# Attention in a fused four-layer kernel: the softmax maxima as contraction rows brought by DMA, and parts stored pair by pair

## The reference

```python
x = x + tanh(g_xattn[0]) * delay_attention(layernorm(x), ctx)
x = x + tanh(g_ffn[0]) * top1_experts(layernorm(x))      # 8 experts
def attention(query, kv):                                # the third layer
    q = (query @ w_q.T).reshape(B, T_q, 16, 8)
    k = (kv @ w_k.T).reshape(B, T_kv, 16, 8)
    v = (kv @ w_v.T).reshape(B, T_kv, 16, 8)
    attn = softmax(einsum('bqhd,bkhd->bhqk', q, k) * 8 ** -0.5, axis=-1)
    return einsum('bhqk,bkhd->bqhd', attn, v).reshape(B, T_q, 128) @ w_o.T
x = x + tanh(g_xattn[1]) * attention(layernorm(x), ctx)
x = x + tanh(g_ffn[1]) * top2_experts(layernorm(x))      # 8 experts
```

## Time and profile before

| | |
|---|---|
| median of 3 runs | 371.15 us (360.84, 371.15, 374.12) |
| profiled execution | 360.57 us |
| its span, first to last instruction | 358.8 us |
| PE busy / DVE / ACT / POOL | 299.6 / 199.5 / 119.0 / 155.1 us |
| mean granted clock of TensorE | 0.92 of full speed |
| experts of the second layer end | 134 us into the span |
| first scores of the attention loop | 157.1 us |
| last addition to x of the attention | 253.2 us |

### The profile page before, as it was taken

One profiled execution on the slowest core, in us unless ns is written; L12 is line 12 of the kernel. 1 busy time (PEld: TensorE's weight loads), 2 busy tenths in 40 slices (PEclk: granted clock), 3 DMA queues, 4 the chain that ended last, 5 costly groups with the idle time before them and its releaser, 6 DMA issues.

```text
span 358.8 us, 8553 instructions
## 1 busy us (share of the span) xinstructions
PE 299.6 (83%) x3060; PEld 253.8 (71%) x3060; DVE 199.5 (56%) x602; ACT 119.0 (33%) x268; POOL 155.1 (43%) x330
## 2 busy tenths in 40 slices
PE   6799978799999983646899899998138999999990
PEld 2556668599999981234688788885125999989980
DVE  4826859344444443723586566663793566656650
ACT  1234144111221110226556455555320333323320
POOL 8550000777776431164364344341017417775521
PEclk9699997999999996969999999999655999999996
DMA  7907995269999964061396959911147999999900
GB/s 204 354 2 207 405 303 172 60 234 266 389 400 310 223 132 132 26 133 18 92 161 132 139 125 142 213 47 32 29 119 256 316 339 399 357 322 300 333 24 7
DMA packets 55023, 70.47 MB, mean 196 GB/s; under 512 B 4555, under 2 KB 44918, under 8 KB 54982
## 3 DMA queue, kind: packets, MB, share of 16 engines
q1 hardware_dynamic: 48006, 59.63, 55.2%
q0 software_dynamic: 3664, 8.73, 9.6%
q10 hardware_dynamic: 3312, 1.58, 1.7%
HBM read 58.95 MB, written 10.96 MB: 195 GB/s over the span
## 4 chain that ended last, share of the span: by engine, by line
PE 55%; DVE 14%; DMA 14%; issue 5%; SPq 4%; ACT 3%; POOL 3%; POOLq 0%; DVEq 0%; ACTq 0%
PE bank L1147 7%; PE bank L974 6%; PE pairA L964 5%; PE pairB L964 5%; PE pairB L1137 4%; DMA qs<-rows_d_d,inv_i 4%; PE pairA L1137 4%; DMA qs<-qparts_d 3%; PE pairB L1490 3%; PE pairA L1481 3%; PE pairB L1491 3%; PE bank L1506 3%; DMA qparts_d<-parts 3%; SPq L1441 2%; SPq L1262 2%
## 5 line engine op out<-in xcount | busy, mean ns | idle before, releaser
L1563 DVE TENSOR_REDUCE maxi<-pairA 128x8 f32<-128x1024 f32 x32 | 39.0, 1220 | 27.5 <-PE pairA L1481 27.3
L1543 ACT ACTIVATE prob<-pairB 128x1024 f32<-128x1024 f32 x32 | 32.8, 1024 | 33.9 <-PE pairB L1491 33.9
L1043 POOL DMA_INDIRECT qs<-rows_b_d,inv_i x23 | 22.4, 973 | 44.0 <-DVE inv_i L723 37.4
L1147 PE MATMUL bank<-wring,prob 128*128 128x128 f32 x312 | 41.3, 276 | 0.0
L1147 PEld LDWEIGHTS bank<-wring,prob 128*128 128x128 f32 x312 | 37.9, 192 | 0.0
L1491 PE MATMUL pairB<-mrow,pick 72*128 72x128 bf16 x256 | 32.0, 219 | 0.0
L1048 POOL DMA_INDIRECT back_d<-ysb,inv_i x23 | 22.6, 984 | 16.8 <-DVE ysb L1009 15.0
L1232 POOL DMA_INDIRECT out_x<-qs,inv_i x16 | 15.8, 987 | 27.1 <-DVE qs L1196 24.9
L1222 POOL DMA_INDIRECT qs<-rows_d_d,inv_i x16 | 15.5, 968 | 27.8 <-DVE inv_i L787 23.2
L1598 POOL TENSOR_TENSOR mparts<-zeros,maxi 128x8 bf16<-128x8 f32 x32 | 7.6, 237 | 41.9 <-DVE maxi L1563 41.9
L1490 PE MATMUL pairB<-qs,ks 72*128 72x128 bf16 x192 | 24.1, 219 | 1.2 <-ACT mrow L1548 1.2
(11 more groups left out here) (306 smaller groups left out, 667.1 us busy)
## 6 DMA issues: line engine op xcount, KB each, us to landing
wring<-in_wts SPq DMA_DIRECT2D x39, 514.0 KB, 7.0
wring<-in_wts SPq DMA_DIRECT2D x23, 768.0 KB, 7.4
ks<-kparts_d SPq DMA_DIRECT2D x18, 192.0 KB
qs<-qparts_d SPq DMA_DIRECT2D x18, 192.0 KB
kparts_d<-parts SPq DMA_DIRECT2D x4, 384.0 KB, 4.0
ctx_s<-kparts_d SPq DMA_DIRECT2D x6, 192.0 KB
qparts_d<-parts SPq DMA_DIRECT2D x3, 384.0 KB, 7.0
ctxT<-qparts_d SPq DMA_DIRECT2D x6, 192.0 KB
```

The costliest lines, as they stand in the source:

```text
L1043: eng.indirect_dma_start(out=xt[:, t.x, :], out_offset=None, in_=rows_d["b"], in_offset=bass.IndirectOffsetOnAxis(ap=inv_i[:, 0, t.k:t.k + ...
L1147: j = eng.matmul(bank[1 + i % 2][:, 0:D], act[:, i % 2, c_, :], wring[:, i % RW, o:o + D], start=(c_ == 0), stop=(c_ == C1 - 1))
L1543: eng.activation(prob[:, at.half(2), :, :].rearrange("p h t -> p (h t)"), pairB[:, :, :].rearrange("p a t -> p (a t)"), ACT.Exp)\
L1563: eng.reduce_max(maxi[:, at.half(0), :], pairA[:, :, :].rearrange("p a (h t) -> p (a h) t", t=T), AX).then_inc(s("mx"), 1)
```

## The change

- `pick` and its 8 matmuls per unit go. The three parts of the negated maxima become contraction rows 72 to 74 (`SM` = 75) of the query side: for each unit SP sends `mrow` (now 24 x 128) by a DMA into rows 72 to 74 of the slot (`rows_of`). The key side has ones there (`ONES` read as two bf16), set by a memset for slots 0 and 1 and copied by DMA to the others (`load_ones`).
- Transposed scores move from two to four steps behind the scores, and what follows them moves by two steps (`LAG` 9 to 11). `mparts` and `mrow` have four buffers.
- Five slots for pairs. Slots 3 and 4 lie in `wring`, the ring of expert weights, and their keys are loaded after the experts of the second layer.
- `kparts_d` and `qparts_d` have one block for each pair, so that a load is 24 rows of 4096 contiguous bf16; writes are one DMA for each pair and go in runs of 256 bf16. SP's list weaves writes, loads and `rows_of` by unit.
- Ahead of the loop: 17 DVE instructions for the inverse deviation become 7 (`spread`) plus a power and a product on POOL (`root`); statistics are taken in another order; a first exponential of one column goes ahead of the norms on ACT; the warm matmuls are 44 and 20 (10 and 14 before), and the 44 no longer wait for x. The norms of chunks 2 to 4 are given to other engines and steps, and the work of these chunks to other steps.

```diff
+    SM = SK + PARTS
+    ROWS = 4
...
-    WARM = (20, 22, 30, 10, 10, 14, 2, 3, 2, 4)
+    WARM = (20, 22, 30, 10, 44, 20, 2, 3, 2, 4)
...
-        kparts_d = scratch("kparts_d", (2 * PARTS - 1, HD * H, NTOK), bf16)
-        qparts_d = scratch("qparts_d", (PARTS, HD * H, NTOK), bf16)
+        kparts_d = scratch("kparts_d", (NB // 2, 2 * PARTS - 1, HD * H, 2 * T), bf16)
+        qparts_d = scratch("qparts_d", (NB // 2, PARTS, HD * H, 2 * T), bf16)
...
-        pick = sb("pick", [SK, HU, T], bf16)
...
-        mparts = sb("mparts", [128, 2, SK], bf16)
-        mrow = sb("mrow", [SK, 2, T], bf16)
+        mparts = sb("mparts", [128, ROWS, PARTS * HU], bf16)
+        mrow = sb("mrow", [PARTS * HU, ROWS, T], bf16)
...
+        def spread(eng, c, lo, hi):
+
+            me, mo, ve, vo = (st[:, lo:hi, k] for k in (1, 4, 2, 5))
+            less, diff, total, var, u, mean = (lnv[:, k, lo:hi] for k in (0, 1, 2, 4, 5, 6))
+            eng.tensor_tensor(diff, me, mo, ALU.subtract)
+            eng.tensor_tensor(total, me, mo, ALU.add)
+            c.link(eng.scalar_tensor_tensor(var, ve, D * EPS, vo, ALU.add, ALU.add))
+            eng.tensor_scalar(mean, total, 0.5, None, ALU.mult)
+            eng.tensor_scalar(less, total, -0.5, None, ALU.mult)
+            c.link(eng.scalar_tensor_tensor(u, diff, 0.25, diff, ALU.mult, ALU.mult))
+            eng.scalar_tensor_tensor(var, var, 1.0 / D, u, ALU.mult, ALU.add).then_inc(s("spread"), 1)
+
+        def root(eng, nth, lo, hi):
+
+            eng.wait_ge(s("spread"), nth)
+            eng.tensor_tensor(lnv[:, 3, lo:hi], lnv[:, 4, lo:hi], neg_half[:, lo:hi], ALU.pow).then_inc(s("root"), 1)
+            eng.wait_ge(s("root"), nth)
+            eng.tensor_tensor(lnv[:, 7, lo:hi], lnv[:, 0, lo:hi], lnv[:, 3, lo:hi], ALU.mult).then_inc(s("rstd"), 1)
...
-        SLOTS = 3
+        SLOTS = 5
...
+        spare_ring = wring[:, 2:RW, :].rearrange("p r w -> p (r w)")
+        spare_slot = [wide(spare_ring[:, n * H * T:(n + 1) * H * T]) for n in range(4)]
+
+        qslot = [qs[0:SM, 0, :, :], qs[0:SM, 1, :, :], wide(ctxT[:, :]), spare_slot[0], spare_slot[1]]
+        kslot = [ks[0:SM, 0, :, :], ks[0:SM, 1, :, :], wide(ctx_s[:, :, :].rearrange("p b d -> p (b d)")), spare_slot[2], spare_slot[3]]
+
+        def load_ones(eng, slot):
+            eng.dma_start(kslot[slot][SK:SM, :, :], kslot[0][SK:SM, :, :]).then_inc(s("ones"), 16)
...
+        def load_rows(eng, slot, parts_d, pair, step):
+
+            for j in range(PARTS):
+                v = parts_d[pair, j * step:j * step + PARTS].rearrange("i (d h) t -> (i d) (h t)", h=H)
+                rows = slot[pair % SLOTS][j * PARTS * HD:(j + 1) * PARTS * HD, :, :]
+                eng.dma_start(rows.rearrange("p h t -> p (h t)"), v).then_inc(s(f"qk{pair % SLOTS}"), 16)
...
-            for j in range(PARTS):
-                v = kparts_d[j:j + PARTS].rearrange("i (d h) t -> (i d) h t", h=H)[:, :, pair * 2 * T:(pair + 1) * 2 * T]
-                eng.dma_start(kslot[pair % SLOTS][j * PARTS * HD:(j + 1) * PARTS * HD, :, :], v).then_inc(s(f"qk{pair % SLOTS}"), 16)
...
+            eng.activation(gt[:, 0, 0:1], zeros[:, 0:1], ACT.Exp)
...
             c.link(take(0))
-            rstd(eng, c, RSTD_C0, 0, GB)
+            spread(eng, c, 0, GB)
+            take(1)
+            eng.wait_ge(s("root"), 1)
             norm_dve(eng, 0).then_inc(s("xnD"), 1)
             norm_dve(eng, 2).then_inc(s("xnD"), 1)
-            take(1)
+            take(2)
+            c.link(take(3))
             q_rest(eng, 0)
-            take(2)
+            q_third(eng, 0)
             q_rest(eng, 1)
-            q_third(eng, 0)
-            c.link(take(3))
+            spread(eng, c, GB, NB)
             q_third(eng, 1)
-            rstd(eng, c, RSTD_C, GB, NB)
+            eng.wait_ge(s("root"), 2)
+            norm_dve(eng, 4).then_inc(s("xnD"), 1)
+            norm_dve(eng, 5).then_inc(s("xnD"), 1)
         DV.append(q_dve)
 
 
 
-        LAG = 9
+        LAG = 11
...
-                eng.dma_start(qparts_d[:, :, b * T:b * T + w].rearrange("i p t -> p i t"), parts[:, g, :, mine]).then_inc(s(f"qparts{k}"), 16)
-
-            def load_queries(pair):
-                v = qparts_d.rearrange("i (d h) t -> (i d) h t", h=H)[:, :, pair * 2 * T:(pair + 1) * 2 * T]
-                for j in range(PARTS):
-                    eng.dma_start(qslot[pair % SLOTS][j * PARTS * HD:(j + 1) * PARTS * HD, :, :], v).then_inc(s(f"qk{pair % SLOTS}"), 16)
-
-            for pair in range(2):
-                write(pair)
-                eng.wait_ge(s(f"qparts{pair}"), 16)
-                load_queries(pair)
-            write(2)
-            eng.wait_ge(s("qparts2"), 16)
-            load_queries(2)
-            for pair in range(SLOTS, NB // 2):
-                if pair % 2 == 0:
-                    write(pair // 2 + 1)
-                    eng.wait_ge(s(f"qparts{pair // 2 + 1}"), 16)
-                wait(eng, s("ST"), (pair - SLOTS + 1) * 4)
-                load_keys(eng, pair)
-                load_queries(pair)
+                for q in range(n // 2):
+                    at_ = mine.start + q * 2 * T
+                    eng.dma_start(qparts_d[b // 2 + q].rearrange("i p t -> p i t"), parts[:, g, :, at_:at_ + 2 * T]).then_inc(s(f"qparts{k}"), 16)
+
+            def written(k):
+                eng.wait_ge(s(f"qparts{k}"), 16 * (CHUNKS[k][1] // 2))
+
+            def slot_free(pair):
+                eng.wait_ge(s("ST"), (pair - SLOTS + 1) * 4)
+
+            def rows_of(n):
+                pair, off, u = n // 4, (n // 2) % 2 * T, n % 2
+                eng.wait_ge(s("mrow"), n + 1)
+                eng.dma_start(qslot[pair % SLOTS][SK:SM, u * HU:(u + 1) * HU, off:off + T], mrow[:, n % ROWS, :]).then_inc(s(f"mrow_in{n % ROWS}"), 16)
+
+            for slot in (3, 4):
+                load_ones(eng, slot)
+                load_keys(eng, slot)
+            for k in range(FIRST_CHUNKS):
+                write(k)
+                written(k)
+                load_queries(eng, k)
+
+            for n in range(NU):
+                rows_of(n)
+                if n == 1:
+                    write(2)
+                if n == 3:
+                    written(2)
+                    load_queries(eng, 2)
+                    load_queries(eng, 3)
+                if n == 5:
+                    write(3)
+                if n == 7:
+                    written(3)
+                    load_queries(eng, 4)
+                if n == 8:
+                    write(4)
+                if n == 9:
+                    slot_free(5)
+                    load_queries(eng, 5)
+                    load_keys(eng, 5)
+                if n == 11:
+                    written(4)
+                    slot_free(6)
+                    load_queries(eng, 6)
+                    load_keys(eng, 6)
+                if n == 15:
+                    slot_free(7)
+                    load_queries(eng, 7)
+                    load_keys(eng, 7)
...
+                    for h, q_, k_ in heads(at.unit(0), SK):
                         i = eng.matmul(pairA[:, h // 4, (h % 4) * T:(h % 4 + 1) * T], q_, k_, start=True, stop=True)
                     i.then_inc(s("S"), 1)
-                    if at.u < 2:
-                        warm(eng, bank[1], WARM[6])
-                if at.on(2):
-                    wait(eng, s("mrow"), at.unit(1))
-                    wait(eng, s("P"), at.unit(2))
-                    for h, q_, k_ in heads(at.unit(2)):
-                        o = pairB[:, h // 4, (h % 4) * T:(h % 4 + 1) * T]
-                        eng.matmul(o, k_, q_, start=True, stop=False)
-                        i = eng.matmul(o, pick[:, h, :], mrow[:, at.half(2), :], start=False, stop=True)
+                    if at.u < 4:
+                        warm(eng, bank[7], WARM[6])
+                if at.on(4):
+                    eng.wait_ge(s(f"mrow_in{at.unit(4) % ROWS}"), 16 * (at.unit(4) // ROWS + 1))
+                    wait(eng, s("P"), at.unit(4))
+                    for h, q_, k_ in heads(at.unit(4), SM):
+                        i = eng.matmul(pairB[:, h // 4, (h % 4) * T:(h % 4 + 1) * T], k_, q_, start=True, stop=True)
                     i.then_inc(s("ST"), 1)
...
```

301 lines of the change are left out of this document (158 added, 143 removed).

## The result

| | changed | before, same chips |
|---|---|---|
| median | 369.22 us (367.31 to 376.06, 4 runs) | 366.00 us (359.72 to 374.12, 4 runs) |
| ratio, 95% interval | 1.0223 [1.0164, 1.0283] | |
| profiled execution, its span | 368.98, 367.1 us | 360.57, 358.8 us |
| granted clock, mean | 0.879 | 0.920 |
| first maximum of the loop to the last | 156.93 to 246.70: 89.8 us | 158.26 to 241.84: 83.6 us |

The ratio compares undisturbed executions only (367.31 to 369.46 us against some 360), so it is larger than that of the two medians, and a kernel further down has no ratio where too few of its executions were undisturbed.

A forecast was written before the change was run, and what follows sets the result against it. PE's instruction list was taken to bound the loop. Savings of 11.2, 6.7 and 4.4 us less losses of 1.5 and 1.8 gave 19.0; from the median 371.15 that is 352.2, forecast as 350 us, range 338 to 357.

The forecast's parts named there:

- Steady unit: Loop from unit 10 on: without the `pick` matmuls a unit takes 2.05 us instead of 2.455, saving 11.2 us.
- Rival 2: Loop: pairA and DVE do not interlock as thought, a unit stays at 2.3 us, total 357 us; chance 0.15.
- rival 4: Loop not bound by PE's list, so removing `pick` frees nothing; total 365 us; chance 0.04.
- The small DMAs: 32 new 6 KB transfers in the loop, mostly hidden by the lag of steps; 1.5 us lost, bounds 0 and 12.
- rival 1: Loop queue: long rows drain no faster, small DMAs behind loads lose 12 us, not 1.5; total 364; chance 0.08.
- rival 3: Loop: PE, idle more often waiting for DMA rows, falls to half clock; 389 us with 20 such units; chance 0.05.
- Units 0 to 10: Loop's first units: 22.6 us from maximum to maximum instead of 29.3, saving 6.7 us, bounds 2 and 9.
- Ahead of the loop: From the experts' end to the first scores: these come at 152.7 instead of 157.1, saving 4.4 us, bounds 1 and 6.
- First write at 147.2: Ahead of the loop: first write of query parts at 147.2 instead of 148.78, from gains of 0.6 and 1.0 us.
- through by 146.5: Ahead of the loop: keys of slots 3 and 4, at 270 GB/s and more, finish just before the first write.
- Tail: After the last scores: values two steps later put the last exponential at 7.95 us instead of 6.2; 1.8 us lost.
- The start from the median of 371.15: Base for the whole kernel: median of three earlier runs, less 19.0 us gives 352.2, set a little lower at 350.

The follow-up runs named there:

- e7: e5 with its spread loads for pairs 4 to 7 on SP's queue again, each behind the rows of maxima of its step; 353.48 us, ratio 0.975.
- e11: Changed kernel with only the loads for pairs 4 to 7 issued one at a time on SP's queue; 378.74 us on a slow-memory chip (kernel before: 393.97).
- e3: Changed kernel with 16, 6 and 10 warm matmuls ahead of the transposed scores in steps 14, 15 and 16; 369.15 us, ratio 1.014.
- e1: Changed kernel with 46 instead of 20 warm matmuls between chunk 1's last product and the first scores; 367.51 us.
- e5: Changed kernel with 46 warm matmuls ahead of the first scores and loads for pairs 4 to 7 spread evenly over steps on ACT's queue; 358.47 us.
- e6: e5 with the keys of slots 3 and 4 moved from ahead of the first query write to steps 1 to 6 on ACT's queue; 351.62 us, ratio 0.969.
- e12: e13 with the set of six query loads for pairs 2 and 3 also taken apart; 351.36 us, ratio 0.963.
- e13: e5 with 6 and 4 more filler matmuls in steps 2 and 3; 352.98 us, ratio 0.969.

## Why the prediction was wrong

**Steady unit, 2.05 us: right.** 2.045 at full clock. (Two slips in its working did no harm: 188.38 to 189.11 is 0.73, not 0.63, and the changed kernel's PE takes 0.61 for the same work; and of DVE's terms 2.77 + 1.27 = 4.04 is what gives 4.05, while the text names the 1.27 twice.) Rival 2 (2.3 us) and rival 4 (nothing gained) are out. The 11.2 us of the term assumed that clock for 21 units; units 10 to 31 took 59.6 us in place of 43.1.

**The small DMAs, 1.5 us: this step failed**, and first in its rate. "Rows of 8 KB are nearest to weights" and "at some 270 GB/s six loads need 4.3 us" rested on the length of a piece. With nothing beside them such loads move 158 GB/s, pieces of 512 bytes 147, and in the loop all DMAs together moved 158, from 189.54 to 207.29. The weights' rows differed from the loads' in two things, length and 128 partitions against 24, and I named only one as "the visible difference". With that, rival 1's condition held. It was priced at 12 us of waits: 6 for the two sets at n = 9 and 11, which came (3.55 and 2.24), and 3 each at n = 3 and 15, which didn't. The one at n = 3 comes, as 1.86 to 3.64 us, in the kernels whose first units run at full clock. Rival 1 ended at 364 and "same". That the sets ahead of the small DMAs cause the waits is shown, by e7 and e11, which send the same loads one at a time. That loads at 270 GB/s would have hidden them is not: no kernel was run with faster loads.

**The clock, rival 3, given 0.05: the larger price.** Half clock behind those waits made units of 3.2 and 3.9 us in turn, some 3.5 where I had put 4.0. Units 10 to 31 took 16.5 us more than forecast, of which the two waits are 5.8 and half clock most of the other 10.7. I worked out its price but took the two rivals as independent; in the traces a fall of the clock follows each wait for rows of 1.86 us or more but one (1.88 us in e3, with 1.00 from 182 to 190). Spreading the loads removed both, 9 to 14 us of loop (e1 against e7 and e5). The argument that the clock had never fallen in the loop before said nothing of a loop that waits.

**Units 0 to 10, 22.6 us: missed.** 30.2. Half clock from 166 to 178 is the larger part: maxima 3 to 8 took 17.2 us, and 11.7 to 12.0 in the four kernels whose clock held with the same instructions there. Another 1.6 lie between maxima 0 and 3, which took 8.9 us at a mean clock of 0.67 (156 to 166) and 7.3 in e1, at a clock of 1.00 (158 to 166). Why the clock falls from maximum 3 on in some traces and not in others stays open. (The 3.1 us by which the text puts the old 29.3 above ten steady units is 4.8; no term uses it.)

**Ahead of the loop.** First write at 147.2: it was issued 10.15 us behind x's first load, 11.59 before, so 1.4 of the 1.6 us came. POOL's powers took 1.05 and 2.39 us, where I had bounded one at 0.2 to 1.5; DVE waited 0.39 and 2.17 for them, and the second isn't ahead of the first write. The write took 4.51 us in place of "2.03 as before", because the keys of slots 3 and 4 were not through by 146.5 (e6: 2.06 without them, e5: 5.27 with them). Even at 270 GB/s the 2.2 MB from 139 us on would have ended at 147.1, not 146.5. Issue of three loads fell from 2.38 to 1.11, as forecast; from the last issue to the landing they took 4.73, not 2.3. Counted from x's first load, which came 1.60 us earlier in this execution, the first scores stand 20.29 us behind it, 19.95 before: 1.44 gained up to the write, 2.48 lost in it, 0.70 gained in issue and loads. Of the 4.4 us nothing is left. The failed step here is "through by 146.5", again the rate of 270 GB/s, and with it "2.3" for the landing of the loads.

**Tail, 1.8 us lost: nearly right.** The last exponential started 8.35 us after the last scores (254.37 - 246.02), forecast 7.95, so 2.15 are lost; the four rounds are 1.81 us apart, not 1.72. The other 1.3 us behind the last maximum lie in the fourth layer, where kernels with this same tail differ by more among themselves (98.3 us in e12 and 101.1 in e5 from the first matmul behind the tail to the end).

**The start from the median of 371.15** was one of three runs that spread over 13 us; with more runs the kernel before has medians of 366 beside the change, 362 to 369 beside three groups of experiments and 394 beside the fourth. So the base was a few us too high. The forecast of 350 missed by 19.2 us, while the sum from the profiled execution, 341.6 against 368.98, missed by 27.4: that the error looks smaller is luck.

## What to carry to other kernels

Before a transfer is priced by a faster one in the trace, list everything in which the two differ; which partitions it covers counts here far more than the length of a piece. A small DMA on which an engine waits must not stand behind a set of loads: send loads one at a time between them, in the same queue if need be. When a wait of a few us is priced, price the units behind it at half clock as well, and after each repair look for the next wait, since a loop that runs faster reaches its loads sooner. Before a difference between two traces is given to an edit, look whether it lies where the edit can reach.

## Not expected of the hardware

- Transfers to few partitions were slow whatever engines took part: 16 rows at a time 141 GB/s, 24 rows 149 to 182, 48 rows 150 to 187, 128 rows 303; but 32 rows 214, beside 208 for 96.
- A small DMA of 6 KB landed 10.88 us after its issue behind twelve loads of 192 KB.
- The same instructions with the same pauses of PE (1.57 us) were followed by half clock in e5 and by full clock in e7, 17.3 against 11.7 us for five units.
- A wait of 1.86 us in e13 was followed by a clock of 0.51 over 16 us, and units 8 to 16 took 8.8 us longer than in e5.
- A power on GpSimd took 1.05 us for 4 columns and 2.39 us for 12, a product of the same size 0.2.
- One chip moved 286 to 297 GB/s from 76 to 113 us, while expert weights load, where the others moved 344 to 354; the kernel before had 394 us there.
